# A state space layer on one core: inputs of two scans in four row strips, vector work behind the pairs, a corrected logarithm and a flat convolution

## The reference, cut to what matters

```
xz = xt @ in_proj                       # (512 sequences, 32 steps, 128) -> 2 x 256 channels
xc, z = xz[..., :256], xz[..., 256:]
xconv = conv_b + sum_k conv_w[:, k] * pad(xc)[:, k:k + T, :]      # 4 taps in time
xc = silu(xconv)
dbc = xc @ x_proj                       # time step (rank 8), B (16 states), C (16 states)
dt = softplus(dbc[..., :8] @ dt_w + dt_b)
dA = exp(dt[..., None] * A)             # A = -exp(A_log), (256, 16)
dBx = (dt * xc)[..., None] * B
h_t = dA_t * h_{t-1} + dBx_t ;  y_t = sum_s h_t * C_t             # the scan over 32 steps
y = (y + Dp * xc) * silu(z)
out = layernorm(xt + y @ out_w + out_b)
```

## Time and profile before

| | us |
|---|---|
| median of three runs | 4235.98 |
| span of the profiled execution | 4229.6 |
| PE busy (83%) | 3512.6 |
| DVE busy (75%) | 3183.5 |
| ACT busy (63%) | 2645.9 |
| POOL busy (59%) | 2493.4 |

### The profile page before, as it was taken

How to read it: one execution, slowest core, us unless ns; L and a number is a source line. 1 busy time by engine, 2 the same in 40 slices (tenths; PEclk the granted TensorE clock), 3 DMA queues, 4 the chain that set the end, 5 groups by cost and what they waited for, 6 DMA issues and landing times. The chain is left out here.

```text
span 4229.6 us, 82803 instructions
## 1 busy us (share of the span) xinstructions
PE 3512.6 (83%) x29152; PEld 2284.8 (54%) x29152; DVE 3183.5 (75%) x6184; ACT 2645.9 (63%) x5169; POOL 2493.4 (59%) x2879
## 2 busy tenths in 40 slices
PE   7998599999999999999999979668884885668566
PEld 4766255555555555555555546436663652357546
DVE  3999388888888888888888856648985856159754
ACT  5887477877877777787778722015765627148552
POOL 3898378788778878877887520006875413025750
PEclk8999599999999999999999976677776877789788
DMA  3000100000000000000000042251000001710233
GB/s 85 24 27 26 37 4 11 21 22 15 18 21 22 11 21 22 14 18 21 21 11 19 16 105 73 77 192 29 26 6 5 1 1 42 251 35 1 75 86 115
DMA packets 271007, 172.54 MB, mean 41 GB/s; under 512 B 41648, under 2 KB 249976, under 8 KB 268536
## 3 DMA queue, kind: packets, MB, share of 16 engines
q1 hardware_dynamic: 270600, 167.25, 13.8%
HBM read 116.59 MB, written 50.60 MB: 40 GB/s over the span
## 5 line engine op out<-in xcount | busy, mean ns | idle before, releaser
L1177 DVE TENSOR_TENSOR_SCAN mam_hs<-mam_dA,mam_ps_b 128x1024 f32<-128x1024 f32 x512 | 1156.2, 2274 | 2.4 <-PE mam_ps_b L965 2.1
L979 PEld LDWEIGHTS mam_ps_h<-mam_ident,mam_hs 128*128 128x128 f32 x4096 | 462.3, 146 | 425.3 <-issue 421.0
L965 PE MATMUL mam_ps_b<-mam_DB,mam_dtxt 32*128 32x512 f32 x2048 | 589.3, 651 | 83.0 <-DVE mam_hs L1177 79.5
L1105 ACT ACTIVATE mam_dA<-mam_dt,mam_A 128x496 f32<-128x496 f32 x1024 | 649.5, 704 | 0.7
L1113 ACT COPY mam_hTb<-mam_ps_h 128x512 f32<-128x512 f32 x768 | 424.9, 583 | 323.7 <-PE mam_ps_h L979 319.8
L979 PE MATMUL mam_ps_h<-mam_ident,mam_hs 128*128 128x128 f32 x4096 | 587.7, 289 | 28.1 <-ACT mam_hTb L1113 26.6
L1187 DVE COPY mam_hTb<-mam_ps_h 128x512 f32<-128x512 f32 x256 | 175.8, 687 | 179.0 <-PE mam_ps_h L979 179.0
L763 POOL TENSOR_SCALAR mam_tap<-mam_xcp,mam_cw 128x512 f32<-128x512 f32 x180 | 282.5, 1569 | 17.6
L991 PE MATMUL mam_ps_y<-mam_hTb,mam_WC 128*32 128x128 f32 x8192 | 280.3, 278 | 0.4 <-issue 0.4
L991 PEld LDWEIGHTS mam_ps_y<-mam_hTb,mam_WC 128*32 128x32 f32 x8192 | 211.6, 110 | 123.1 <-issue 94.5
L965 PEld LDWEIGHTS mam_ps_b<-mam_DB,mam_dtxt 32*128 32x128 f32 x2048 | 157.9, 186 | 220.4 <-issue 217.2
(11 more groups left out here) (724 smaller groups left out, 8569.5 us busy)
## 6 DMA issues: line engine op xcount, KB each, us to landing
moe_wg<-in_L_ffn_weight SPq DMA_DIRECT2D x32, 1024.0 KB, 7.7
rnn_xr<-x SPq DMA_DIRECT2D x23, 512.0 KB, 6.0
l1y_wh<-mode_weights SPq DMA_DIRECT2D x16, 544.0 KB, 3.7
gat_hg<-in_x SPq DMA_DIRECT2D x16, 512.0 KB, 7.3
h<-gat_out SPq DMA_DIRECT2D x32, 256.0 KB, 2.3
mam_ht<-h SPq DMA_DIRECT2D x128, 64.0 KB, 2.0
mam_hr<-h SPq DMA_DIRECT2D x128, 64.0 KB, 2.1
mam_xt<-in_x SPq DMA_DIRECT2D x128, 64.0 KB, 2.0
```

Of the source, the lines that this page charges most:

```text
L965: last = pe.matmul(ps_b[w % 2][:, n, :], steps[r, g * P:(g + 1) * P], DB[r, g, :, :].rearrange("p s t -> p (s t)"), start=True, stop=True, ...
L979: last = pe.transpose(ps_h[n][:, q * P:(q + 1) * P], hs[:, w % 3, c:c + P], ident[:, :])
L1105: act.activation(dA[:, h, :, n, 1:], dt[:, i % 2, h, :].rearrange("p (q t) -> p q t", q=Q)[:, :, 1:], ACT.Exp, scale=A[:, h, n:n + 1]).the ...
L1177: dve.tensor_tensor_scan(hs[:, w % 3, :], dA[:, h, first:first + 2, :, :].rearrange("p q s t -> p (q s t)"), ps_b[w % 2][:, :, :].rearrang ...
```

## The change

- `inputs` is issued once for a pair of units. Its four products go to four row strips and to the four banks of one buffer `ps_b`. It waits for both scans of the pair before; there is no second buffer. It stands last in PE's odd slots, and `sums` stands first in the even ones.
- DVE's slot begins with `scan(w)`. The copy and all other vector work stand in odd slots, behind the second scan of a pair.
- `states_of_input` and `c_in` move from DVE to ACT.
- The polynomial, `choose` and the tiles `po` and `small` are gone. DVE rounds `1 + e` (`one_more`), POOL adds `e` to `relu(v)` (`plus`), ACT takes the logarithm of the rounded sum, DVE works out what the rounding lost (`lost`), and POOL subtracts it. These steps are spread over more slots and cross a turn's border.
- The convolution runs over 557 columns in one stretch, over the pads too, into a new tile `cv`, which `silu_x` reads; it waits for `silu_x` of the turn before.
- The steps of a turn on PE, ACT and POOL have other slots, and waits that fit them. `finish` comes ten slots earlier. No transfer is added or moved in SP's order.

```diff
+    V = U // 2
+    NP = Q * PADT
...
-        ps_b = [s.ps(f"ps_b{j}", (P, 2, N)) for j in range(2)]
+        ps_b = s.ps("ps_b", (P, J, N))
...
             def convolve(i, h):
+                L = NP - K + 1
...
-                acc = xs[:, i % 3, h, :].rearrange("p (q t) -> p q t", q=Q)
-                step(pool.tensor_scalar(acc, xcp[:, h, :, 0:T], cw[:, h, 0:1], None, ALU.mult))
+                acc = cv[:, h, 0:L]
+                step(pool.tensor_scalar(acc, xcp[:, h, 0:L], cw[:, h, 0:1], None, ALU.mult))
                 for k in range(1, K):
...
+                    step(pool.tensor_scalar(tap[:, 0:L], xcp[:, h, k:k + L], cw[:, h, k:k + 1], None, ALU.mult))
+                    step(pool.tensor_tensor(acc, acc, tap[:, 0:L], ALU.add))
...
+            def plus(i, h):
...
+                pool.tensor_tensor(dt[:, i % 2, h, :], dt[:, i % 2, h, :], e[:, h, :], ALU.add
+                                   ).then_inc(plus_ready, 1)
...
+                pool.tensor_tensor(dt[:, i % 2, h, :], ln[:, h, :], e[:, h, :], ALU.subtract
+                                   ).then_inc(dt_ready, 1)
...
# pool, order of the slots
+                if u == 0 and turn(k):
+                    spread_c(k, 2)
+                if u == 1:
+                    if turn(k + 2) and k + 2 >= EARLY:
+                        convolve(k + 2, 0)
+                    if turn(k + 1):
+                        plus(k + 1, 1)
+                if u == 4:
+                    if turn(k - 1):
+                        gate(k - 1, 0)
+                        gate(k - 1, 1)
+                    if turn(k + 2) and k + 2 >= EARLY:
+                        convolve(k + 2, 1)
+                if u == 7:
...
+                if u in (9, 11, 13, 15) and turn(k + 1):
+                    spread_b(k + 1, (u - 9) // 2)
+                if u in (9, 10) and turn(k + 1):
+                    time_steps(k + 1, u - 9)
...
# tensor
+            def inputs(p):
+                i, v = divmod(p, V)
+                h, g = divmod(v, G)
                 pe.wait_ge(DB_ready, i * G + g + 1)
                 pe.wait_ge(dx1_ready if h else dx0_ready, i + 1)
...
+                pe.wait_ge(scanned, 2 * p)
                 steps = dtxt1[:, i % 2, :] if h else dtxt0[:, i % 2, :]
...
+                for j in range(J):
+                    r = slice(j * T, (j + 1) * T)
+                    last = pe.matmul(ps_b[:, j, :], steps[r, g * P:(g + 1) * P],
                                      DB[r, g, :, :].rearrange("p s t -> p (s t)"), start=True, stop=True,
...
+                                     tile_position=(j * T, 0))
...
+                if u % 2 == 0 and pair(w // 2 - 2):
+                    sums(w // 2 - 2)
                 if unit(w - 1):
                     flip(w - 1)
...
+                if u in (0, 2) and turn(k + 2):
+                    project_x(k + 2, u // 2)
+                if u in (1, 3) and turn(k - 1):
+                    turn_sums(k - 1, u // 2)
+                if u in (4, 6) and turn(k + 2):
+                    gate(k + 2, (u - 4) // 2)
+                if u == 7 and turn(k + 3):
+                    turn_tokens(k + 3)
+                if u == 8 and turn(k - 1):
+                    project_out(k - 1)
+                if u == 10 and turn(k + 2):
+                    project_bc(k + 2)
+                if u == 11 and turn(k + 1):
                     split_c(k + 1)
...
+                if u in (12, 14) and turn(k + 2):
+                    time_steps(k + 2, (u - 12) // 2)
+                if u in (13, 15) and turn(k + 1):
+                    turn_steps(k + 1, (u - 13) // 2)
+                if u % 2 == 1 and pair((w + 1) // 2):
+                    inputs((w + 1) // 2)
...
# tensor, waits of two steps of a turn
             def split_c(i):
...
+                pe.wait_ge(bc_ready, min(i + 2, TURNS))
...
             def turn_steps(i, h):
                 pe.wait_ge(dtx_ready, 2 * i + h + 1)
...
+                pe.wait_ge(dt_read, min(2 * i + 3 + h, 2 * TURNS))
...
# scalar
             def logarithms(i):
...
                 for h in range(HV):
...
+                    act.wait_ge(rest_ready, 2 * i + h + 1)
+                    act.activation(ln[:, h, :], ln[:, h, :], ACT.Ln).then_inc(ln_ready, 1)
...
+            first1, first0 = (0, 3, 6, 9, 12, 16), (0, 2, 6, 9, 11, 14, 16)
...
+                if u == 8:
+                    if turn(k + 3):
+                        tokens_in(k + 3)
+                    if turn(k + 2):
+                        silu_x(k + 2, 0)
+                        silu_x(k + 2, 1)
+                if u == 9 and turn(k + 1):
+                    logarithms(k + 1)
+                if u == 11 and turn(k + 2):
+                    states_of_input(k + 2)
+                if u in (13, 15) and turn(k + 2):
+                    softplus(k + 2, (u - 13) // 2)
                 if unit(w - 1):
                     states_in(w - 1, 0)
...
# vector
+            def one_more(i, h):
...
+                TS(ln[:, h, :], e[:, h, :], 1.0, None, ALU.add).then_inc(e1_ready, 1)
...
+            def lost(i, h):
...
+                STT(out=e[:, h, :], in0=ln[:, h, :], scalar=1.0, in1=dt[:, i % 2, h, :], op0=ALU.subtract,
+                    op1=ALU.subtract).then_inc(rest_ready, 1)
...
             for w in SLOTS:
                 k, u = divmod(w, U)
...
+                if unit(w):
+                    scan(w)
+                if u % 2 == 1 and unit(w - 1):
+                    states_in(w - 1)
                 if u == 1 and turn(k - 1):
                     take_y(k - 1, 0)
...
                 if u == 3 and turn(k - 1):
                     take_y(k - 1, 1)
...
+                if u == 5 and turn(k + 1):
+                    lost(k + 1, 0)
+                    one_more(k + 1, 1)
+                if u == 7 and turn(k + 1):
+                    lost(k + 1, 1)
+                if u == 9 and turn(k - 1):
                     residual(k - 1)
                 if u == 11 and turn(k - 1):
                     moments(k - 1)
                 if u == 13 and turn(k - 1):
                     scale(k - 1)
...
+                if u == 15 and turn(k + 2):
+                    one_more(k + 2, 0)
```

More of the change, by code:

```diff
@@ L645, in mamba @@
         dtx = s.sb("dtx", [P, HV, N])
-        e, ln, po = (s.sb(n, [P, HV, N]) for n in ("e", "ln", "po"))
-        small = s.sb("small", [P, HV, N], u8)
+        e, ln = (s.sb(n, [P, HV, N]) for n in ("e", "ln"))
         bt, ct = s.sb("bt", [P, 2, G, S]), s.sb("ct", [P, 2, G, S])
@@ L744, in _ @@
             step(pool.memset(half_c[:, :], -0.5))
[L745 removed]
+            step(pool.memset(xcp[:, :, :], 0.0))
             step(pool.memset(dA[:, :, :, :, 0:1], 0.0))
@@ L833, in _ @@
[L833 to L838, removed]
-                if u == 4 and turn(k + 2) and k + 2 >= EARLY:
-                    convolve(k + 2, 1)
-                if u == 8 and turn(k - 2):
-                    finish(k - 2)
+                if u in (9, 11, 13, 15) and turn(k + 1):
+                    spread_b(k + 1, (u - 9) // 2)
@@ L851, in _ @@
+                if u == 14 and turn(k - 1):
+                    finish(k - 1)
                 if u == 15 and turn(k + 2):
-                    time_steps(k + 2, 0)
+                    plus(k + 2, 0)
         @block.tensor
@@ L899, in time_steps @@
             def time_steps(i, h):
-                pe.wait_ge(bc_ready, i + 1)
-                pe.wait_ge(dt_read, 2 * i + h)
+                pe.wait_ge(xs_ready, 2 * i + 2)
+                if h == 0:
+                    pe.wait_ge(bc_ready, i + 1)
+                    pe.wait_ge(cp_ready, i)
+                else:
+                    pe.wait_ge(dt_read, 2 * i + 1)
+                    pe.wait_ge(dx0_ready, i)
                 pe.wait_ge(folded, 4)
@@ L1061, in silu_x @@
                     act.wait_ge(conv_first, 2 * i + h + 1)
-                act.activation(xs[:, i % 3, h, :], xs[:, i % 3, h, :], ACT.Silu, bias=cb[:, h:h + 1]
+                if i >= 3:
+                    act.wait_ge(y_taken, 2 * (i - 3) + h + 1)
+                act.activation(nodes(xs[:, i % 3, h, :]), nodes(cv[:, h, :])[:, :, 0:T], ACT.Silu, bias=cb[:, h:h + 1]
                                ).then_inc(xs_ready, 1)
@@ L1144, in _ @@
                 if 10 <= u and turn(k + 1):
                     decays(k + 1, 0, first0[u - 10], first0[u - 9] - first0[u - 10])
-                if u in (12, 13) and turn(k + 2):
-                    softplus(k + 2, u - 12)
-                if u == 13 and turn(k + 2):
-                    logarithms(k + 2)
-                if u == 15 and turn(k + 3):
-                    tokens_in(k + 3)
         @block.vector
@@ L1270, in _ @@
                     scale(k - 1)
-                if u in (14, 15) and turn(k + 2):
-                    choose(k + 2, u - 14)
+                if u == 15 and turn(k + 2):
+                    one_more(k + 2, 0)
 NKY, NKX = 32, 17
```

235 lines of the change are left out of this document (87 added, 148 removed).

## The result

The changed kernel takes 4131.61 us (four runs, 4124.43 to 4132.23) beside 4235.68 of the kernel before, a ratio of 0.9765 (0.9734 to 0.9795). It is faster by 104 us where 218 were forecast, and 1.6 us above the upper end of the range. The profiled execution has a span of 4130.2 us, 99.4 less than before.

The account below looks back on a forecast made before the run. PE, with DVE close behind, was taken to bound the stage. DVE's 48.2 + 0.5 + 4.7 + 0.8 = 54.2 us a turn against 61.0, times 32, saves 218 us: 4018 us, range 3910 to 4130.

Parts of the forecast that it names:

- Rival 2: POOL's convolution stays slow, 1.71 us a product, holding ACT's `silu_x` up by 2 us: 56.4 us a turn, 4089; chance 0.12.
- The single buffer: `inputs` of a pair waits for both scans before; other DVE work just covers some 1.3 us; 0.5 us a turn added.
- the late slots: PE's slots 11, 13, 15: `split_c` and `turn_steps` wait for ACT, delaying `inputs`; 1.1, 1.8, 1.8 us open, together 4.7.
- Rival 1: Stalls are hidden because ACT runs ahead: 51.5 us a turn, time 3932; chance 0.18.
- Rival 3: PE's clock falls more often, waiting for each pair's second scan: 57 us a turn, time 4108; chance 0.10.
- Rival 4: Four row strips take as long as two pairs, 2.12 us, uncovered by the single buffer: slower, 4316; chance 0.08.
- The ends: Before the first scan and after the last: nothing put; earlier `finish` spares at most a few us after the last scan.

Follow-up runs that it names:

- the strips alone: Kernel before with only the four strips (inputs once a pair, last in PE's odd slots, one buffer), DVE's order, softplus and convolution unchanged: 4282.16 us, ratio 1.0130.
- the fast run: Changed kernel with POOL's convolution back on rows (512 columns) and each product written as two operations (times weight, plus 0.0): 3932.11 us, ratio 0.9299.

## Why the prediction was wrong

- **The step that failed** is POOL's convolution: "Line 769, a flat tile, has 0.622 us ... I take 0.75, at the near end." The product measured 1.775 us (median 1.683). Two rows with several differences were compared (shape, constant or weight, number of operations), and the price was given to the one that the change made. The runs show the third in its place: on the same flat columns with the same weights, two operations take 0.735 us and one 1.683. Rival 2 (chance 0.12), the far bound of that term, is what happened: product 1.77 where it said 1.71. Its reason was wrong as well, as the weight costs 0.075 us. That the product with two operations lies at 0.735, beside the 0.75 taken, is luck: the change had one operation.
- **The price of a slow product was also too small.** Rival 2 gave 2 us a turn for the wait and 56.4 for the turn; measured are waits of 6.5 us of ACT and 5.2 of DVE and a turn of 58.2. The forecast's convolution, flat with 0.735 us a product, is the run with two operations on flat columns: its turn is 52.4 us, so the slow product costs 5.8 us a turn, some 180 us in all. That run, 3950.16 us, lies 68 us below the forecast and in its range: from 600 to 2000 us it has 45.8 us of PE, 47.5 of DVE, 46.2 of ACT and 40.9 of POOL a turn, where 48.5, 48.2, 46.8 and 41.2 were put, and DVE is idle for 4.9 where 6.0 were put.
- PE: right. Four strips 1.07 us (1.16 taken), PE 47.4 us (48.5). By the Trainium skill, "TensorE: Matmul & The Clock Gate", on packing small matmuls, four row strips bring 3.07; here they bring 0.95 x 4 / 1.07 = 3.55, so the measured row decides.
- DVE: right in sum (47.7 for 48.2). `one_more` 0.958 us mean for 0.98, `lost` 0.969 for 1.2. ACT: right; function loads are three a turn.
- The single buffer and the late slots: 4.6 us before scans where 0.5 + 4.7 were put, and 4.1 a turn in the fast run (110.8 us before scans in 27.0 turns). The sum is near in part by luck: the three late slots have 0.41, 1.14 and 2.25 us for 1.1, 1.8 and 1.8, the rest lies before slots 8 and 10, and the largest ends with ACT's decays and not with the inputs.
- Rival 1 (stalls hidden, 51.5 us a turn) is nearer than 54.2 to what the fast convolution gives, 51.9 on rows, but not by hidden stalls: DVE is busy for 1265.1 of 1400 us in that run, 46.9 us of a turn where 48.2 were put, and idle for 5.0 where 6.0 were.
- Rival 3 (clock): 0.96 granted, as before, so nothing more was lost than before; only the strips alone went lower, to 0.93 (600 to 2200 us). Rival 4 falls by the 1.07 us; the part of it that puts a single buffer with nothing to cover it is what DVE's 8.4 us a turn with the strips alone look like. Its 57.8 should read 57.6 (7.2 x 8), and the 51 to 57.5 us of the range are narrower than its terms (46 + 1 to 50 + 8); neither moves the forecast.
- The ends: the first scan came 11.9 us earlier, where nothing was put. Which step of the start gave that was not looked into.

## What to carry to other kernels

When a price is taken from another line, list all that differs between the two lines (shape, kind of operand, number of operations), and bound by each of them; one cheap run settles what an argument can't. An engine with slack on average can still set the time by one long stretch of work, if another engine waits for its end ahead of work that everyone needs. And an undone part can look worthless while something else is the bound: four strips, with their buffer and place, were worth nothing measurable with the slow convolution and some 100 us with the fast one. Last, the engine that a profile names as the releaser of a wait with several conditions need not be the last one: the ends of the instructions settle it.

## What was not expected of the hardware

- On GpSimd a `tensor_scalar` with one operation took 1.57 us for 512 float32 columns, and with a second operation (plus 0.0) 0.70; in the kernel before the same edit took it from 1.57 to 0.70 too. Constants in place of weights saved 0.075 us, rows of 32 out of 35 columns cost nothing beyond their columns. The Trainium skill, "GPSIMD Engine Reference", on elementwise cycle accounting, gives about 0.77 us as the best for 512 elements; the form with two operations is a little better, the one with a single operation takes twice that.
- On GpSimd a product of two tensors of 512 columns of which one is repeated took 1.05 us, the one with two full tensors 1.27.
- From 600 to 2000 us PE's granted clock was 1.00 in the run with two operations and 0.96 in the changed kernel, where PE stood up to 3.7 us once a turn and then worked for some us at 1.2 GHz. The length of one wait doesn't tell it: in one turn of the run with two operations PE stood 0.94 us and the products behind it took 2.09 us at a granted clock of 0.50, and 16 us later it stood 1.14 us and the same products took 1.14.
